# Attention context divided in feature-major form, with its parts picked apart by DMAs

## The reference

```python
q, k, v = (heads(xn @ W.T + b) for W, b in ((Wq, bq), (Wk, bk), (Wv, bv)))   # 16 heads of 8
scores = (einsum('bhqd,bhkd->bhqk', q, k) + rel_shift(einsum('bhqd,ld->bhql', q + u, r))) * 8 ** -0.5
p = softmax(where(mask, NEG, scores))           # causal
ctx = einsum('bhqk,bhkd->bhqd', p, v)           # back to (b, s, 128)
h = h + ctx @ Wo.T + bo
h = h + gelu(ln(h) @ W1.T + b1) @ W2.T + b2
```

## Time and profile before

| | us |
|---|---|
| median of 3 runs (lowest to highest) | 2341.47 (2340.98 to 2346.53) |
| profiled execution, span from first to last instruction | 2345.2 |
| TensorE busy | 2276.7 (97%) |
| VectorE busy | 1993.9 (85%) |
| ScalarE busy | 1837.2 (78%) |
| POOL busy | 1143.1 (49%) |
| granted TensorE clock, mean of the core | 0.993 |

### The profile page before, as it was taken

How to read it: one execution, slowest core, us unless ns; L and a number is a source line. 1 busy time by engine, 2 the same in 40 slices (tenths; PEclk the granted TensorE clock), 3 DMA queues, 4 the chain that set the end, 5 groups by cost and what they waited for, 6 DMA issues and landing times. The chain is left out here.

```text
span 2345.2 us, 83100 instructions
## 1 busy us (share of the span) xinstructions
PE 2276.7 (97%) x31360; PEld 1974.0 (84%) x31360; DVE 1993.9 (85%) x4943; ACT 1837.2 (78%) x2869; POOL 1143.1 (49%) x2089
## 2 busy tenths in 40 slices
PE   5999999999999999999999999999999999799999
PEld 4788888888888888888888888888888888678787
DVE  6899999988888888888888888888888887577775
ACT  2688888888888888888888888888888888655554
POOL 4455555555545554545554455554555544333332
PEclk9899999999999999999999999999999999899999
DMA  5344433333333333333333333333333332011100
GB/s 142 105 117 108 111 93 89 86 92 87 94 93 92 87 91 90 94 93 85 89 88 97 94 91 84 92 87 94 92 103 91 89 92 61 21 28 28 28 24 19
DMA packets 227432, 196.04 MB, mean 84 GB/s; under 512 B 29025, under 2 KB 225761, under 8 KB 227041
## 3 DMA queue, kind: packets, MB, share of 16 engines
q1 hardware_dynamic: 227040, 190.73, 30.3%
HBM read 14.46 MB, written 4.19 MB: 8 GB/s over the span
## 5 line engine op out<-in xcount | busy, mean ns | idle before, releaser
L1000 DVE TENSOR_REDUCE rowmax<-bank 128x4 f32<-128x1024 f32 (+1 forms) x768 | 915.4, 1219 | 106.8 <-PE bank L575 74.0
L816 ACT ACTIVATE probs<-bank 128x1024 f32<-128x1024 f32 x768 | 737.6, 1024 | 84.2 <-PE bank L635 83.5
L635 PE MATMUL bank<-qstack,kstack 64*128 64x128 f32 (+1 forms) x4096 | 423.5, 299 | 4.4 <-DMA qstack<-maxrows 4.4
L575 PE MATMUL bank<-kstack,qstack 62*128 62x256 f32 (+1 forms) x4096 | 418.4, 301 | 7.6 <-DMA qstack<-base 7.6
L857 ACT ACT_TABLE_LOAD x256 | 328.4, 1283 | 4.5
L575 PEld LDWEIGHTS bank<-kstack,qstack 62*128 62x128 f32 x4096 | 317.4, 193 | 8.0 <-issue 8.0
L635 PEld LDWEIGHTS bank<-qstack,kstack 64*128 64x128 f32 x4096 | 315.7, 192 | 5.3 <-DMA qstack<-maxrows 5.3
L1176 POOL CAST xn1T_parts<-xn1T 128x256 fp32r<-128x256 f32 x128 | 50.8, 397 | 484.6 <-ACT xn1T L824 484.6
L597 PE MATMUL bank<-maskT_half,pick_half 64*128 64x128 bf16 (+1 forms) x3072 | 267.9, 241 | 10.8 <-DVE turn_c L969 2.1
L724 PE MATMUL bank<-w,hidden 128*128 128x128 f32 x2048 | 271.7, 276 | 2.6 <-ACT hidden L866 2.6
L655 PE MATMUL bank<-probs,v_pad 128*32 128x256 f32 x4096 | 271.0, 382 | 0.6 <-DVE v_tok L981 0.6
(11 more groups left out here) (153 smaller groups left out, 5184.7 us busy)
## 6 DMA issues: line engine op xcount, KB each, us to landing
qstack<-base SPq DMA_DIRECT2D x768, 128.0 KB, 2.5
kstack<-base SPq DMA_DIRECT2D x384, 128.0 KB, 2.5
turn_x<-turn_c SPq DMA_DIRECT2D x512, 32.0 KB, 1.9
qstack<-maxrows SPq DMA_DIRECT2D x256, 16.0 KB
out<-ot SPq DMA_DIRECT2D x16, 256.0 KB, 2.4
h_all<-in_x SPq DMA_DIRECT2D x7, 512.0 KB, 5.2
xin<-in_x SPq DMA_DIRECT2D x14, 256.0 KB, 3.1
w<-in_w SPq DMA_DIRECT2D x8, 256.0 KB, 3.1
```

The lines of the kernel that those rows point to most:

```text
L575: last = pe.matmul(bank[:, b0 + b, i * wide:(i + 1) * wide], qstack[rows, r, p0 + i, t * 128:(t + 1) * 128], kstack[rows, r, p0 + i, 0:wid ...
L635: last = pe.matmul(bank[:, b0 + b, i * wide:(i + 1) * wide], kstack[rows, r, p0 + i, kt * 128:(kt + 1) * 128], qstack[rows, r, p0 + i, q0: ...
L816: act.activation(probs[:, k], bank[:, A_BANK[k]:A_BANK[k] + 2, :], ACT.Exp, scale=SCALE).then_inc(exp_done[k], 1)
L1000: dve.tensor_reduce(rowmax[:, n % 2, t, :, p0:p0 + heads], bank[:, M_BANK[k]:M_BANK[k] + 2, :].rearrange("p b (h c) -> p b h c", h=heads), ...
```

## The change

The context stays feature-major. In v_pad the ones no longer stand in the ninth column of a head but in every second one: values in the even columns, ones in the odd. So each value's row of ctxT_raw has its denominator in the row behind it. Two DMAs of 64 rows of 1 KB gather the odd rows to ctx_den, two the even rows to ctx_num. ScalarE makes the inverse in place as exp(-ln(x)), POOL multiplies ctx_num by it in place, and b3 reads ctx_num. The six transposes, the divide and the copy to ctxT go. The Ln and the exponentials are in one table set, and tables are loaded by name, without probes.

In SyncE's slot the context's four DMAs stand between content(s) and exchange(s); the exchange is now behind the content in slots 0 and 1 as well. base is double-buffered by tile, with the rotated queries in a tile of their own, and "rotated" is written in place in turn_x. x0 of the experts is loaded into w_1, after the last split of it.

```diff
             def exchange(n):
                 sp.wait_ge(cosines_used, n + 1)
-                at_least(sp, rot_ready, n)
+                at_least(sp, rot_rest, n)
...
+            def context(n):
+
+                sp.wait_ge(context_out, n + 1)
+                at_least(sp, ctxT_ready, n)
+                for g in range(2):
+                    sp.dma_start(ctx_den[64 * g:64 * g + 64], ctxT_raw[1:128:2, g]).then_inc(den_landed, 16)
+                at_least(sp, proj_done, n)
+                for g in range(2):
+                    sp.dma_start(ctx_num[64 * g:64 * g + 64], ctxT_raw[0:128:2, g]).then_inc(num_landed, 16)
...
-                if live(s) and s < EXCHANGES_FIRST:
-                    exchange(s)
                 if live(s):
                     content(s)
-                if live(s) and s >= EXCHANGES_FIRST:
+                if live(s - 4):
+                    context(s - 4)
+                if live(s):
                     exchange(s)
...
-                if live(s - 4):
-                    b1(s - 4)
...
-                if live(s - 4):
-                    b2(s - 4)
...
             def split_first(n):
                 act.wait_ge(qk_done, n + 1)
-                if n > 0:
-
-                    act.wait_ge(stack_landed[(n - 1) % RING], 16 * STACK_DMAS * ((n - 1) // RING + 1))
+                if n > 1:
+
+                    act.wait_ge(stack_landed[(n - 2) % RING], 16 * STACK_DMAS * ((n - 2) // RING + 1))
...
-            def ctxT_out(n):
-                act.wait_ge(ctx_turned, n + 1)
-                at_least(act, proj_done, n)
-                act.copy(ctxT[:], bank[:, CTX_BANK, 0:S]).then_inc(ctxT_ready, 1)
...
+            def inverse(n):
+
+                act.wait_ge(den_landed, 32 * (n + 1))
+                act.activation(ctx_den[:], ctx_den[:], ACT.Ln).then_inc(log_ready, 1)
+                act.wait_ge(log_ready, n + 1)
+                act.activation(ctx_den[:], ctx_den[:], ACT.Exp, scale=-1.0).then_inc(inv_ready, 1)
...
-                if live(s - 5):
-                    ctxT_out(s - 5)
                 if live(s - 6):
                     xn2T_out(s - 6)
+                if live(s - 5):
+                    inverse(s - 5)
                 if live(s - 4):
                     exp_round(s - 4, 1)
...
-                    load_table(2 * (s - 6), ACT.Gelu)
+                    act.preload_act_table_set(GELU_SET)
                     gelu(s - 6)
-                    load_table(2 * (s - 6) + 1, ACT.Exp)
+                    act.preload_act_table_set(EXP_SET)
...
+            def normalize_context(n):
+
+                pool.wait_ge(inv_ready, n + 1)
+                pool.wait_ge(num_landed, 32 * (n + 1))
+                pool.tensor_tensor(ctx_num[:], ctx_num[:], ctx_den[:], ALU.mult).then_inc(ctxT_ready, 1)
...
                 if live(s - 6):
                     xn2_split(s - 6)
+                if live(s - 5):
+                    normalize_context(s - 5)
                 if live(s - 1):
                     turned(s - 1)
```

More of the change, by code:

```diff
@@ L81 @@
 HIGH, LOW = 3.0e38, -3.0e38
+EXP_SET, GELU_SET = "natural_log_exp_and_others", "gelu_and_others"
 def wait_alone(eng, sem, value, apart):
@@ L250, in layers_program @@
         turn_x = sb("turn_x", [128, S])
-        rotated = sb("rotated", [128, S])
-        base = sb("base", [128, 2, 3, S], F32R)
+        base = sb("base", [128, 2, 2, 2, S], F32R)
+        base_turned = sb("base_turned", [128, 2, S], F32R)
         v_tok = sb("v_tok", [128, VR, T, D])
@@ L266, in layers_program @@
         ctxT_raw = sb("ctxT_raw", [128, 2, S])
-        rsum = sb("rsum", [128, T * H])
-        ctx_tok = sb("ctx_tok", [128, T * D])
-        ctxT = sb("ctxT", [128, S])
+        ctx_num = sb("ctx_num", [128, S])
+        ctx_den = sb("ctx_den", [128, S])
         stats2 = sb("stats2", [128, T, 6])
@@ L460, in turned_content @@
                 for c in range(NP):
-                    sp.dma_start(qstack[NP + c:128:LANE, r].bitcast(F32), base[:, PARTS_Q[c], 2].bitcast(F32)
+                    sp.dma_start(qstack[NP + c:128:LANE, r].bitcast(F32), base_turned[:, PARTS_Q[c]].bitcast(F32)
                                  ).then_inc(rot_landed[r], 16)
@@ L665, in pv @@
                 last.then_inc(context_done[half], 1)
[L667 to L682, removed]
             def b3(n):
@@ L687, in b3 @@
                     pe.wait_ge(middle_landed, 16 * MIDDLE_DMAS)
-                bank_left(pe, (live(n + 3), max_done[4], n + 4), (live(n), ctxT_ready, n + 1))
+                bank_left(pe, (live(n + 3), max_done[4], n + 4), (live(n + 1), exp_done[4], n + 2),
+                          (live(n - 1), h1_ready, n))
                 for t in range(T):
-                    last = pe.matmul(bank[:, PROJ_BANK, t * 128:(t + 1) * 128], ctxT[:, t * 128:(t + 1) * 128],
+                    last = pe.matmul(bank[:, PROJ_BANK, t * 128:(t + 1) * 128], ctx_num[:, t * 128:(t + 1) * 128],
                                      w_o[:, layer(n)], start=True, stop=True)
@@ L834, in split_first @@
                 act.wait_ge(qk_done, n + 1)
-                if n > 0:
-                    act.wait_ge(stack_landed[(n - 1) % RING], 16 * STACK_DMAS * ((n - 1) // RING + 1))
+                if n > 1:
+                    act.wait_ge(stack_landed[(n - 2) % RING], 16 * STACK_DMAS * ((n - 2) // RING + 1))
                 for src in range(2):
-                    last = act.activation(base[:, 0, src], bank[:, QK_BANK, src * S:(src + 1) * S], ACT.Identity,
+                    last = act.activation(base[:, n % 2, 0, src], bank[:, QK_BANK, src * S:(src + 1) * S], ACT.Identity,
                                           bias=b_cols[:, layer(n), src:src + 1])
@@ L988, in split_rest @@
                 for src in range(2):
-                    last = dve.scalar_tensor_tensor(base[:, 1, src], bank[:, QK_BANK, src * S:(src + 1) * S],
+                    last = dve.scalar_tensor_tensor(base[:, n % 2, 1, src], bank[:, QK_BANK, src * S:(src + 1) * S],
                                                     b_cols[:, layer(n), src:src + 1],
-                                                    base[:, 0, src].bitcast(F32), ALU.add, ALU.subtract)
+                                                    base[:, n % 2, 0, src].bitcast(F32), ALU.add, ALU.subtract)
                 last.then_inc(qk_rest, 1)
@@ L1018, in maxrows_out @@
                 dve.tensor_copy(maxrows[:], bank[0:2 * H, ROWS_BANK, 0:S]).then_inc(maxrows_ready, 1)
[L1020 to L1029, removed]
             def resid_1(n):
@@ L1040, in experts_stats @@
                 dve.wait_ge(h2_ready, N - B + 2)
-                dve.tensor_tensor(h, ex.x0[:], h, ALU.add).then_inc(ex.x1_ready, 1)
+                dve.tensor_tensor(h, w_1[:].rearrange("p (c d) -> p c d", c=GT), h, ALU.add).then_inc(ex.x1_ready, 1)
                 dve.wait_ge(ex.x1_ready, 1)
@@ L1193, in turned @@
                 at_least(pool, rot_rest, n)
-                pool.tensor_tensor(rotated[:], turn_s[:], turn_x[:], ALU.add).then_inc(rot_ready, 1)
+                pool.tensor_tensor(turn_x[:], turn_s[:], turn_x[:], ALU.add).then_inc(rot_ready, 1)
                 pool.wait_ge(rot_ready, n + 1)
```

45 lines of the change are left out of this document (19 added, 26 removed).

## The result

The changed kernel takes 2539.5 us (median of 4 runs, 2523.7 to 2551.4) against 2341.2; the ratio is 1.083, 95% interval 1.080 to 1.086. It is slower by 198 us where 119 were forecast, and outside the range. The direction and the main mechanism were right, the size was not.

A forecast was written before the change was run, and what follows sets the result against it. TensorE, 97% busy, bounds the kernel, with SyncE and POOL's ring close behind; the change makes that ring set the period: 124 x (16.2 - 15.26) = 117, plus 5 start, less 3 drain, +119: 2460 us, range 2355 to 2520.

The forecast's parts named there:

- The ring of SyncE and POOL: Line 461, maxima, content, exchange, landing, POOL's rotation, next line 461: 13.53 us against a 15.32 slot, slack 1.79.
- The pair of Ln and Exp: On ScalarE between xn2T and the first exponential: costs TensorE 0.95 us a slot there, between 0.75 and 1.15.
- the second rival: TensorE's gain from six fewer transposes shows: 128 x 0.71 = -91, 2250 us; 4% whole, 4% for part.
- I take 16.2: SyncE's ring after the change, in us a slot: 13.53 + 2.53 = 16.06, plus 0.2 for stalls.
- the stalls added by 4/15: SyncE's queue: about one 0.79 us stall a slot; 19 issues for 15 add 4/15 of it, 0.2.
- TensorE (15.5) fits inside 16.2 and shows up as waiting: TensorE's slot, 15.26 - 0.71 + 0.95 = 15.5 us, stays within the ring's 16.2 and adds nothing to the period.
- The ring is longer: Third rival: a second queue stall each slot or stretched landings, 16.9 us and more, +203, 2545 us; 8%.
- context_out comes in time for the four issues: On SyncE's queue: context_out comes at 1219.97 + 0.57, before the content is through; new waits cost 0.05 us.
- The start: Slots 0 and 1: exchange behind content, 3.9 us later, passed on one to two times; 5 us taken (0 to 8).
- Base's second buffer: Frees line 839 from a wait on the stack's DMAs, which had long landed: counted as nothing.
- the table loads: On ScalarE: stay two per slot at 1.28 us, counted as nothing.
- the product on POOL: One 128x256 product, 0.73 us, ahead of the rotation: fits idle time, counted nothing; 0.73 if the exchange lands in time.

The follow-up runs named there:

- run 1: Kernel before plus four 64 KB DMAs in SyncE's queue between content and exchange, nothing else of the change: 2521.8 us against 2345.2, ratio 1.075.
- run 2: Kernel before plus the same four 64 KB DMAs, placed behind the exchange: 2352.1 us against 2345.2, ratio 1.003.
- run 3: Kernel before plus two 64 KB DMAs instead of four, between content and exchange: 2381.3 us against 2344.5, ratio 1.016.
- run 6: Changed kernel with the context's four DMAs issued on POOL's queue, behind its bias rows: 2344.2 us against 2344.5 for the kernel before, ratio 0.999.
- run 4: Changed kernel with ScalarE's inverse one place later, behind the exponential of round 1; context still ahead of the exchange: 2518.1 us, ratio 1.074 to the kernel before.
- run 10: Changed kernel's SyncE order (content, context, exchange), with the inverse behind all three exponentials and POOL's product behind the rotation: 2504.7 us, ratio 1.068 to the kernel before.
- run 5: Changed kernel with the context's four DMAs behind the exchange, inverse as in the change: 2981.7 us, ratio 1.270 to the kernel before.
- run 9: Changed kernel, all DMAs on SyncE, context's behind the exchange, inverse behind three exponentials, POOL's product behind the rotation: 2306.7 us, ratio 0.984 to the kernel before.
- run 8: Changed kernel, context's DMAs on POOL, inverse behind all three exponentials, POOL's product behind the rotation: 2275.7 us against 2343.6 for the kernel before, ratio 0.971.

## Why the prediction was right in kind and wrong in size

*What stood.* The ring of SyncE and POOL and its slack of under 1.8 us were read from the profile of before, and runs 1, 2 and 3 show them: the place decides, two DMAs nearly fit, four don't. The pair of Ln and Exp, 0.95 in the estimate, delays the exponential by 0.77, within the bounds given; nothing is said by it of the sum, since the ring was longer. The Trainium skill's sentence on initiation time ("DMA: Bandwidth & Descriptors", "Issuing engines are not separate DMA queues") would have led to the second rival. The same section also says that issuing on several engines saves only the sequencer's time. Here, moving the four issues to POOL was worth 195 us (run 6 against the change); that holds the sequencer's time on the ring, and also the earlier landing of the denominators.

*The step that failed, first part: "I take 16.2".* The ring was summed from one slot, with the stalls added by 4/15 and the median for the landing. In the changed kernel's window SyncE's mean slot is 16.84 = 13.07 of issues + 3.51 until the rotation is through + 0.26 until VectorE's split is. The 16.2 hold 12.9 for the first and 3.3 for the second. The mean would have been better for the issues, and it was at hand: SyncE issues for 15.34 - 4.22 - 0.75 = 10.37 us a slot before, 0.69 for each of 15 DMAs; nineteen are 13.1. The 3.3 rest on the median landing of 1.9, while single landings took up to 3.6. The 0.17 and the 0.21 make 124 x 0.38 = 47 us.

*Second part: "TensorE (15.5) fits inside 16.2 and shows up as waiting".* Waiting was taken to be free: the term of 0.26, a TensorE so late that it holds up the content and with it the ring, is missing from the sum. It makes 124 x 0.26 = 32 us. Each of its 13 waits follows a drop of the clock late in the slot before. Here TensorE had stood idle for 2.21 us until 1073.69, the clock was at 0.50 by 1075, and the content waited from 1080.2 to 1081.4:

```profile
1075.00:1076.00 1.00, 1.00 (x12) 0.82 (x10) 0.00 (x0) 0.73 (x1) 0.84 (x2) 0.50 0.00 0
```
```profile
1079.03 1.16 SPq L466 DMA_DIRECT2D qstack<-maxrows  x2
1081.49 0.58 SPq L448 DMA_DIRECT2D qstack<-base  x1
```

How much of the 0.26 is the idle time and how much the clock behind it, no run separates. The drops alone don't do it: runs 1, 4 and 10 have them in 10, 7 and 9 slots, and SyncE waits for the split there for 3.1, 0.4 and 0 us. The forecast never asked what happens when TensorE, 97% busy, begins to wait.

Together 119 + 47 + 32 = 198, the measured difference, but that it fits so well is luck. The 16.84 are a window's mean; the whole run has 16.72, and the kernel before has 15.34 in the window for 15.26. The sum is good to some 10 us. "The ring is longer", the rival with 8%, had the right time (2545) for a reason that didn't occur: in the changed kernel the queue doesn't stall a second time in each slot, and the exchange's median landing is still 1.9. A small slip besides: the upper end of the range, 2341.5 + 124 x 1.44 = 2520, leaves out the start that its sentence names; with it, 2525 would still have been too low.

*A step left out: the landing of the denominators.* The prediction checked that context_out comes in time for the four issues, but not that the denominators land in time for the inverse. That is the second ring. In the change it puts 24.6 us of waits ahead of the inverse, 29 times in the window, and makes drops more frequent (23 slots, against 7 and 9 in runs 4 and 10). Inverse and product late against early (2504.7 against 2539.5) is worth 35 us, close to the 32 of the missing term, and it explains why the context could not simply be moved behind the exchange (2981.7).

*The small terms.* The start: the eighth v_tok addition came at 114.8 us instead of 111.4, which includes three or four slots with the context, so the exchange behind the content cost at most 3.4 us where 5 were forecast. Base's second buffer, the table loads (1283 ns as before) and the product on POOL showed no cost of their own: run 6 has them all and is as fast as the kernel before.

## What to carry to other kernels

Before putting work into a queue, close the loop: what that queue issues last in a period, what waits for its landing, and whether the queue itself waits for that. Idle time of the queue behind its last transfer hides nothing that is put ahead of it; the same work behind it costs next to nothing, as long as nobody needs its data soon (7 us in run 2, 442 more than the change in run 5). If an engine at 97% begins to wait, ask whether the wait and a lower clock behind it make the engine so late that the ring has to wait for it. And if an inserted operation shifts a row of waits, move it behind all whose banks are waited for, not behind the first.

## What the runs showed of the hardware

In the windows from 600 to 1700 us, TensorE had stood idle for 1.4 us or more in one piece shortly before each fall of its granted clock to 0.50 (1.2 GHz), but not each such idle time was followed by a fall. In the kernel before with four more DMAs, a wait of 1.51 us ended at 836.3 and the clock fell within a microsecond; a wait of 2.09 us that ended at 1312.1 passed without:

```profile
835.00:836.00 1.00, 0.00 (x0) 0.00 (x0) 0.90 (x1) 0.00 (x0) 0.71 (x1) 1.00 0.09 27
...
837.00:838.00 1.00, 1.00 (x16) 1.00 (x12) 0.00 (x0) 0.95 (x1) 0.00 (x0) 0.50 0.79 200
...
1311.00:1312.00 1.00, 0.00 (x0) 0.00 (x0) 0.17 (x1) 0.00 (x0) 0.07 (x1) 1.00 0.10 29
1312.00:1313.00 1.00, 0.88 (x20) 0.88 (x22) 0.00 (x0) 0.10 (x1) 0.00 (x0) 1.00 0.75 190
```

What decides between the two was not tried and stays open. That it falls after idleness at all agrees with the Trainium skill, "TensorE: Matmul & The Clock Gate", "Part 1: The HAM clock gate (the "warmup" mystery)", which has the gate halve the clock when the array hasn't been busy enough.

Stalls in SyncE's queue come about once a slot, in whichever DMA is just issued; per DMA the mean was 0.69 us before and after. Issues of more than 0.9 us, counted in the window: 65 of 1080 before, 69 of 1241 in the change, 59 of 1241 in run 1, 94 of 1406 in run 9. What they go with isn't shown. POOL's own issues took no longer than SyncE's, but the data landed later, 2.8 us in the median against 2.1 for the denominators' DMAs on SyncE's queue in the changed kernel. In run 8:

```profile
L1177 POOL DMA_DIRECT2D ctx_den<-ctxT_raw x256: 542/583/775, 75.0 to 1948.4; - x128
...
DMA to landing us min/median/max: 1.9/2.8/4.7
```
